# Where two expert biases are added, who adds a tile's first weighted row, and when half a block's stores start

## The reference

```python
combine, dispatch = top2_dispatch(z_g, Wg, C)        # 24 experts, 4 groups of 256 tokens, C = 22
disp = einsum('sec,sd->ecd', dispatch, x)
h    = einsum('ecd,edf->ecf', disp, W1) + b1[:, None, :]     # 128 -> 512
hid  = relu(layer_norm(einsum('sec,ecf->sf', combine, h)))   # back to tokens, normalised
y    = einsum('ecf,efd->ecd', einsum('sec,sf->ecf', dispatch, hid), W2) + b2[:, None, :]
out  = layer_norm(z + einsum('sec,ecd->sd', combine, y))
```

## Time and profile before

| | us |
|---|---|
| three runs | 425.24, 430.27, 430.97 (median 430.27) |
| profiled execution | 429.6 |
| its span on the core | 427.9 |
| granted TensorE clock, mean | 0.941 |
| busy in the span: PE, DVE, ACT, POOL | 381.2, 263.7, 192.8, 117.2 |

### The profile page before, as it was taken

How to read it: one execution, slowest core, us unless ns; L and a number is a source line. 1 busy time by engine, 2 the same in 40 slices (tenths; PEclk the granted TensorE clock), 3 DMA queues, 4 the chain that set the end, 5 groups by cost and what they waited for, 6 DMA issues and landing times.

```text
span 427.9 us, 7077 instructions
## 1 busy us (share of the span) xinstructions
PE 381.2 (89%) x2675; PEld 216.7 (51%) x2675; DVE 263.7 (62%) x682; ACT 192.8 (45%) x303; POOL 117.2 (27%) x160
## 2 busy tenths in 40 slices
PE   8998968999897999999998899987997897999961
PEld 3675447874343232333332585644575332788951
DVE  4777703325788789889823886626168637893435
ACT  5323102310506567776787596655625541533200
POOL 4013785460507146100110000110000055744042
PEclk9995997999999799999999999996899998999976
DMA  4499514014167444000000000005999487322132
GB/s 116 134 141 330 210 44 115 30 44 113 37 185 191 106 121 103 3 1 3 2 3 0 2 1 2 0 0 204 389 294 290 159 264 227 121 79 63 41 81 55
DMA packets 35877, 46.03 MB, mean 108 GB/s; under 512 B 4778, under 2 KB 21682, under 8 KB 35844
## 3 DMA queue, kind: packets, MB, share of 16 engines
q1 hardware_dynamic: 33156, 38.57, 32.0%
q0 software_dynamic: 2688, 7.02, 5.9%
HBM read 31.67 MB, written 13.78 MB: 106 GB/s over the span
## 4 chain that ended last, share of the span: by engine, by line
PE 58%; DVE 12%; issue 8%; DMA 6%; ACT 6%; POOL 4%; another core or an unknown queue 4%; POOLq 0%; SPq 0%; DVEq 0%; ACTq 0%
PE ps L1438 7%; PE ps L1694 7%; PE ps L1680 7%; PE ps L1655 6%; PE ps L1990 4%; PE ps L1663 3%; PE ps L2015 2%; PE ps L1943 2%; PE ps L1852 2%; PE ps L1799 2%; POOL y_d L593 2%; PE ps L1442 2%; PE ps L1808 2%; PE ps L1599 2%
## 5 line engine op out<-in xcount | busy, mean ns | idle before, releaser
L1255 DVE TENSOR_REDUCE early<-ps 128x1 f32<-128x512 f32 x128 | 81.6, 685 | 13.2 <-PE ps L1655 9.8
L812 ACT ACTIVATE R<-ps 128x1024 f32<-128x1024 f32 x64 | 62.6, 1019 | 23.9 <-PE ps L1680 23.0
L1680 PE MATMUL ps<-R 75*128 75x512 bf16 x128 | 38.8, 391 | 2.2 <-DMA R<-R 2.1
L1655 PE MATMUL ps<-R 72*128 72x512 bf16 x112 | 39.2, 392 | 0.8 <-DVE early L1255 0.8
L1438 PEld LDWEIGHTS ps<-ident,R 128*77 128x77 f32 (+1 forms) x216 | 24.2, 145 | 23.1 <-issue 9.9
L663 POOL DMA_INDIRECT R<-h_d,srow x16 | 15.4, 963 | 73.8 <-DMA h_d<-ff 67.6
L1438 PE MATMUL ps<-ident,R 128*77 128x128 f32 (+1 forms) x216 | 31.7, 280 | 4.2 <-ACT R L804 1.8
L1694 PE MATMUL ps<-R,vaug 128*9 128x512 f32 x256 | 34.3, 609 | 0.6 <-ACT R L812 0.6
L1442 PE MATMUL ps<-early,ones_b 128*128 128x512 bf16 (+1 forms) x119 | 30.6, 403 | 1.6 <-POOL ident L532 1.6
L1655 PEld LDWEIGHTS ps<-R 72*128 72x128 bf16 x112 | 11.0, 98 | 32.5 <-DVE early L1255 19.6
L1221 DVE TENSOR_SCALAR R<-ps,vcol 128x256 f32<-128x256 f32 x16 | 7.0, 479 | 25.2 <-remote 13.4
(11 more groups left out here) (340 smaller groups left out, 717.6 us busy)
## 6 DMA issues: line engine op xcount, KB each, us to landing
R<-in_L_ffn_W_dram SPq DMA_DIRECT2D x1, 6144.0 KB, 19.7
h_d<-R SPq DMA_DIRECT2D x12, 256.0 KB, 4.7
q_d<-R SPq DMA_DIRECT2D x24, 96.0 KB, 1.9
R<-k_d SPq DMA_DIRECT2D x24, 96.0 KB
R<-q_d SPq DMA_DIRECT2D x8, 288.0 KB
R<-in_L_ffn_w_dram SPq DMA_DIRECT2D x1, 2048.0 KB
h_d<-ff SPq DMA_DIRECT2D x6, 256.0 KB, 4.6
disp_d<-R SPq DMA_DIRECT2D x1, 1032.0 KB, 13.0
```

What stands on the lines that cost most here:

```text
L812: s.activation(probs[idx % 4], ps[:, 2 * (idx % 2):2 * (idx % 2) + 2, :].rearrange("p b t -> p (b t)"), ACT.Exp, scale=QK_SCALE).then_inc( ...
L1255: v.tensor_reduce(mcol[:, u, col:col + 1], bank(ring_bank("row", n)), AX.X, ALU.max).then_inc(s1_max, 1)
L1655: m.matmul(bank(ring_bank("row", n)), Q9[0:KQ, b, h, t * P:(t + 1) * P], K9[0:KQ, b, h, :], start=True, stop=True).then_inc(s1_mm, 1)
L1680: ins = m.matmul(bank(2 * (idx % 2) + j), K9[0:KM, b, h, kt * P:(kt + 1) * P], Q9[0:KM, b, h, :], start=True, stop=True)
```

## The change

- b1 is added to quads 0 to 11 by DVE as it copies them, from `b1rep`, each expert's row repeated over its 32 slots' partitions (six loads of 256 KB). `DVE_QUADS` is now 0 to 11; the copies stand inside the routing: block 0's after the one-hots, block 1's after the row indices for the gathers. In quads 12 to 17, which ACT copies, PE adds b1 by one bf16 matmul per quad (`quad_bias`: three parts of b1 times `of_slot`, which ACT builds; POOL splits b1 in parts during the attention). `hidden_bias`, the transposes of combine and ACT's copies of them are gone.
- b2 is added by DVE in the copies of output blocks, from `b2rep` (six loads of 64 KB). ACT copies no blocks; `output_bias` and DVE's additions of it are gone.
- SP issues the twelve loads between W1 and W2, after the last projection.
- ACT makes the first weighted row of tiles 1 to 7 in PSUM (`inner_part`); DVE does it for tile 0. The root takes epsilon as its bias, and L1394 is gone.
- SP waits before the store of quad 9 (second half of block 1) until tiles 0 and 1 are gathered.
- POOL splits tile 0 right after the gathers of tile 2, DVE splits tile 1 itself.
- The transposes of the last group's weights stand ahead of the hidden groups. ACT's evacuations and roots are interleaved anew.
- The output groups are finished in the order 0, 3, 1, 2; blocks 1 and 2 are copied by DVE after group 0.

```diff
-DVE_QUADS = (6, 8)
+DVE_QUADS = tuple(range(12))
...
-BIAS_BANK = (5, 4) * 4
-LAST_BANK = (6, 7, 1)
+PART_BANK = (4, 5)
+LAST_BANK = (0, 6, 7)
+KB = 96
...
+        b1rep = [v[:, F1 * i:F1 * (i + 1)] for v in (
+            flat(attn), wx[:, :, :].rearrange("p w d -> p (w d)"), vaug[:, :, :, :].rearrange("p t h d -> p (t h d)")) for i in range(2)]
+        b1_parts = wx_qk[0:KB, :, :].rearrange("p w d -> p (w d)").bitcast(BF16)
+        of_slot = bias[0:KB, R_QV:R_SO + 1, :].rearrange("p r d -> p (r d)").bitcast(BF16)
...
-        out_order = (0, 1, 3, 2)
+        out_order = (0, 3, 1, 2)
...
+            sp.wait_ge(proj_mm, 2 * B)
+            for quad in range(QUADS):
+                sp.dma_start(b1rep[quad], a["L1_ffn_b1"][4 * quad:4 * quad + 4, :].unsqueeze(1).to_broadcast([4, 32, F1])).then_inc(ld_rep, 16)
+            for quad in range(QUADS):
+                sp.dma_start(b2rep[:, D * quad:D * (quad + 1)],
+                             a["L1_ffn_b2"][4 * quad:4 * quad + 4, :].unsqueeze(1).to_broadcast([4, 32, D])).then_inc(ld_rep, 16)
...
+                if blk == 1 and s == 3:
+                    for q in (0, 1):
+                        sp.wait_ge(gathered[paired[q]], 32)
...
-                if q == 3:
+                if q == 2:
                     last_rest(0)
-                    last_rest(1)
...
-                s.activation(tmp8[:, q:q + 1], tmp8b[:, q:q + 1], ACT.Sqrt).then_inc(hstd, 1)
+                s.activation(tmp8[:, q:q + 1], mv[:, q, 1:2], ACT.Sqrt, bias=eps6[:, :]).then_inc(hstd, 1)
+            def inner_part(q):
+                t = paired[q]
+                act.wait_ge(gathered[t], 32)
+                if q == 1:
+                    act.wait_ge(gates_ready, 1)
+                if q >= 2:
+                    act.wait_ge(hvar, q - 1)
+                s.activation(bank(PART_BANK[q % 2]), got1[q % 4][:, 0, :], ACT.Copy, scale=gate[1][:, 0, t:t + 1]).then_inc(hpart, 1)
...
-            for i in range(QUADS):
-                copy_quad(i)
+            act.wait_ge(proj_mm, 2 * B)
+            for part in range(3):
+                rows = slice(32 * part, 32 * part + 32)
+                ins = s.copy(of_slot[rows, :].rearrange("p (e c) -> p e c", c=32),
+                             ident[rows, 32 * part:32 * part + E1].unsqueeze(2).to_broadcast([32, E1, 32]))
+            ins.then_inc(of_slot_ready, 1)
             evac_slots1(2)
-            for b in range(B):
-                act.wait_ge(comb_tp, b + 1)
-                s.copy(combT[:, b * SEQ:(b + 1) * SEQ], ps[0:E1, 4 + b, :]).then_inc(combT_ready, 1)
+            evac_slots1(3)
...
-            def copy_block(blk, part):
-                act.wait_ge(y1_mm, 2 * blk + part + 1 + (B if blk else 0))
-                for half in range(2):
-                    wait_half_stored(act, BLOCKS - 1, half)
-                s.copy(yblock[blk][part], ps[:, BLOCK_BANK[blk] + part, 0:(4, 2)[part] * D]).then_inc(y1_act, 1)
-            def copy_quads(first, last):
-                for i in range(first, last + 1):
-                    copy_quad(i)
-            copy_quad(7)
-            copy_quads(9, 11)
-            evac_slots1(3)
-            copy_quads(12, 13)
+            copy_quad(12)
+            copy_quad(13)
+            inner_part(1)
             hid_std(0)
-            copy_quads(14, 16)
+            copy_quad(14)
+            copy_quad(15)
+            copy_quad(16)
             hid_std(1)
             copy_quad(17)
+            copy_last(0)
+            inner_part(2)
+            evac_hidden(0)
             hid_std(2)
-            for c in range(4):
-                evac_hidden(c)
+            inner_part(3)
+            evac_hidden(1)
+            evac_hidden(2)
             hid_std(3)
-            for i in range(3):
-                copy_last(i)
+            evac_hidden(3)
+            copy_last(1)
+            copy_last(2)
+            inner_part(4)
+            evac_hidden(4)
             hid_std(4)
-            for c in range(4, 7):
-                evac_hidden(c)
+            inner_part(5)
+            evac_hidden(5)
+            evac_hidden(6)
             hid_std(5)
             evac_hidden(7)
+            inner_part(6)
             hid_std(6)
-            copy_block(0, 0)
-            copy_block(0, 1)
+            inner_part(7)
             hid_std(7)
             for c in range(8, 15):
                 evac_hidden(c)
-            copy_block(1, 0)
-            copy_block(1, 1)
             for i, gr in enumerate(out_order):
-                if i == 1:
-                    copy_block(2, 0)
-                    copy_block(2, 1)
...
+            def copy_quads(first, last):
+                dve.wait_ge(ld_rep, 16 * 2 * QUADS)
+                for i in range(first, last):
+                    blk, slot = i // QUADS, i % QUADS
+                    dve.wait_ge(h1_mm, i + 1)
+                    if blk >= 1:
+                        wait_half_stored(dve, blk - 1, slot // 3)
+                    v.tensor_tensor(ring[slot], bank(W1_BANKS[i % 3]), b1rep[slot], ALU.add).then_inc(h1_dve, 1)
...
                     one_hot_slots()
+                    copy_quads(0, QUADS)
...
                     v.tensor_tensor(growh[:, :, :], to_slot, col1, ALU.add).then_inc(grow_ready, 1)
+                    copy_quads(QUADS, 2 * QUADS)
...
+            for q in range(T):
+                t = paired[q]
+                inner, rest = hsum[q % 6], hrest[q % 6]
+                partial = bank(PART_BANK[q % 2])
+                if q == 0:
+                    dve.wait_ge(gathered[t], 32)
+                    me.link(v.tensor_scalar(partial, got1[0][:, 0, :], g1[:, 0, t:t + 1], None, ALU.mult))
+                else:
+                    dve.wait_ge(hpart, q)
+                if q >= 6:
+                    dve.wait_ge(hdisp_mm, 4 * ((q - 6) // 2 + 1))
+                me.link(v.scalar_tensor_tensor(out=inner, in0=got1[q % 4][:, 1, :], scalar=g1[:, 1, t:t + 1],
+                                               in1=partial, op0=ALU.mult, op1=ALU.add))
+                me.link(v.bn_stats(st6[:, q, :], inner))
+                v.bn_aggr(mv[:, q, :], st6[:, q, :]).then_inc(hvar, 1)
+                dve.wait_ge(hstd, q + 1)
+                me.link(v.reciprocal(rstd[:, q:q + 1], tmp8[:, q:q + 1]))
+                me.link(v.tensor_scalar(inner, inner, mv[:, q, 0:1], rstd[:, q:q + 1], ALU.subtract, ALU.mult))
+                v.tensor_tensor(rest, inner, top(inner), ALU.subtract).then_inc(hid_r1, 1)
+                if q == 1:
+                    dve.wait_ge(hid_r1, 2)
+                    v.tensor_tensor(hlast[1], rest, top(rest), ALU.subtract).then_inc(hid_p3, 1)
...
-            for i in DVE_QUADS:
...
-                v.tensor_copy(ring[slot], bank(W1_BANKS[i % 3])).then_inc(h1_dve, 1)
-            for q in range(T):
...
-                dve.wait_ge(hb_mm, q + 1)
...
-                me.link(v.scalar_tensor_tensor(out=partial, in0=got1[q % 4][:, 0, :], scalar=g1[:, 0, t:t + 1],
-                                               in1=partial, op0=ALU.mult, op1=ALU.add))
...
-                v.tensor_scalar(tmp8b[:, q:q + 1], mv[:, q, 1:2], MOE_EPS, None, ALU.add).then_inc(hvar, 1)
...
-            add_bias_rows()
+            def copy_block(blk):
+                for part in range(2):
+                    dve.wait_ge(y1_mm, 2 * blk + part + 1)
+                    for half in range(2):
+                        wait_half_stored(dve, BLOCKS - 1, half)
+                    columns = (4, 2)[part] * D
+                    v.tensor_tensor(yblock[blk][part], ps[:, BLOCK_BANK[blk] + part, 0:columns],
+                                    b2rep[:, 4 * D * part:4 * D * part + columns], ALU.add).then_inc(y1_dve, 1)
+            copy_block(0)
...
+                if i == 1:
+                    ins.then_inc(gates_ready, 1)
+                    dve.wait_ge(gates_ready, 1)
+                else:
+                    me.link(ins)
             for b in range(B):
...
+            def quad_bias(i):
+                wait_quad_copied(pe, i - 3)
+                m.matmul(bank(W1_BANKS[i % 3]), of_slot[:, P * (i % QUADS):P * (i % QUADS + 1)], b1_parts, start=True, stop=False)
...
-            pe.wait_ge(comb_ready, 1)
-            for t in range(T):
-                ins = tp(ps[0:E1, 4 + t // TB, (t % TB) * P:(t % TB + 1) * P], comb[:, t, :], P)
-                if t % TB == TB - 1:
-                    ins.then_inc(comb_tp, 1)
             first_product(1, 0)
             first_product(1, 1)
             dispatch(3)
-            pe.wait_ge(ld_hid, 32)
-            hidden_bias(0)
-            first_product(2, 0)
-            hidden_bias(1)
-            first_product(2, 1)
-            hidden_bias(2)
-            hidden_bias(3)
-            for i in range(BLOCKS * QUADS - 3, BLOCKS * QUADS):
+            pe.wait_ge(bias_parts, 1)
+            pe.wait_ge(of_slot_ready, 1)
+            last = BLOCKS * QUADS
+            for i in range(last - QUADS, last - QUADS + 3):
+                quad_bias(i)
```

(79 more changed lines are left out.)

44 lines of the change are left out of this document (10 added, 34 removed).

## The result

The changed kernel takes 444.22 us (median of four runs, 442.97 to 448.24), the kernel before, run beside it, 430.62 us (median of four). The ratio is 1.037, 95% interval 1.027 to 1.048: slower, where 426.0 us was forecast with a range up to 433.0. The profiled execution took 448.24 us, 3.5 us above the next slowest run.

A forecast was written before the change was run, and what follows sets the result against it. Bound by TensorE, almost without holes from 371.52 us, behind a DMA relay: -3.9 (biases) +0.7 (second group) = -3.2 mid-kernel, -5.1 at the end; 429.6 - 5.1 + 0.7 (median) + 0.8 (waits) = 426.0 us, range 420.5 to 433.0.

The forecast's parts named there:

- The loads of repeated rows: SP's queue between the two weights: twelve loads take 4.1 + 1.3 us, second weights land at 339.1 instead of 333.7.
- The queue: SP's queue: first stores wait behind the second weights, first gather at 344.5 instead of 343.00, +1.5 us.
- Held stores: SP before quad 9: block 1's stores land +4.3 us later, shrunk to +0.7 at the first hidden group.
- rival that the hold becomes the limit: SP before quad 9: second hidden group at 375.5 uses up the 3.9 us gained; 434.4 us, chance 0.10.
- Second group: Second hidden group on TensorE: starts at 372.2 against 371.52, +0.7 us, with VectorE at 3.4 us per tile.
- Middle sum: TensorE from second hidden group to block 1's products: these start at 393.0 against 396.16, -3.2 us.
- The tail: Block 2's products to the end: thin stretch gone, last gathers in time, VectorE ends at 420.6 against 425.67, -5.1 us.
- bursts: Last 18 matmuls of block 2, issued unevenly before the change; forecast to vanish as TensorE ends before the gathers.
- the 4 us: Block 2's products: time lost before the change against 28 ns per matmul, forecast to be won back.
- the thin stretch: TensorE's slow last products of block 2, forecast gone; the rival that it stays gave 431.1 us, chance 0.28.
- the 2.7 of the sum: The 24 sum products at the end: 2.7 us at 2.4 GHz instead of 5.39 at half clock.
- The slower case: Rival with SP's hold before quad 9 as limit and the thin stretch kept: 434.4 us, chance 0.10.

The follow-up runs named there:

- e1: Changed kernel with the same repeated bias rows in 16 loads of slowest dimension 32 instead of 12 of slowest dimension 4: 1.015 of before.
- e2: Changed kernel without SP's wait ahead of quad 9's store: 1.032 of before.
- e3: e1 without SP's wait ahead of quad 9's store: 1.012 of before.
- e12: e9 without SP's wait ahead of quad 9's store: 1.006 of before.
- e8: Kernel before plus only the six b1 loads (slowest dimension 4, data unused) between first and second weights: 1.035 of before.
- e11: Kernel before plus only the b1 rows, unused, in twelve loads of slowest dimension 32 ahead of the second weights: 1.010 of before.
- e5: e1 with VectorE's copies of block 1 ahead of output group 0 instead of behind it: 1.007 of before.
- e9: e5 with the b2 rows loaded behind the stores of block 1 instead of ahead of the second weights: 1.003 of before.

## Why the prediction was wrong

The step that failed is the price of "The loads of repeated rows". It took 1.57 MB at 387 GB/s and 0.39 MB at 295 GB/s, 5.4 us, as if any DMA filled all engines. From the first weights' issue to the second weights' landing the changed kernel took 19.6 us more than before (61.8 against 42.2). The upper bound for the first gather, +5.4, rested on that rate (the lower one, 0, on stores that pass), so the range held no case near the truth. e1 puts 10.2 us of the 19.6 on the form and leaves the rest to the bytes: 1.97 MB, every copy of a row counted (the profile lists 256 KB for a load of four rows of 2 KB), at the 239 GB/s of e1 are 8.2 us. Why these rows of 2 KB go at 239 GB/s and those of the first weights at 387 no run shows. The Trainium skill (DMA: Bandwidth & Descriptors, Why a DMA increments its semaphore by 16 and not by 1, How many engines) says that the slowest dimension of each side that isn't 1 is looked at and the largest number up to 16 that divides both is taken: 4 for `[4, 32, 512]`, 16 for `[32, 2, 512]`. The trace agrees (a share of 0.27 against 1.05 to 1.10). By that rule, as an estimate, the twelve loads come to 4 times the 5.4 us, 21.6, close to the 19.6 measured. It stood in the page I cited for another rule, and the shape stood in the diff.

The other steps, by their own numbers:

- **The queue.** Right: stores wait behind the second weights. With the loads at their true price it passed 14.9 of the 19.6 us on to the first gather, where +1.5 was forecast, and the end came 16.5 us later (table).
- **Held stores.** Right in size: first hidden group 17.4 us after the first gather, 17.3 forecast. The rival that the hold becomes the limit fell (e2, e3, e12).
- **Second group.** 28.7 us after the first gather, 27.7 forecast. VectorE needs 3.4 to 3.6 us per tile, as said. Its wait of 3.37 us for tile 2's weighted row is the gather's: ScalarE had itself waited 4.95 us for the rows, which landed 5.20 us after the second gather's issue, where the prediction took 3.6 to 4.2. The wait of 2.62 us for tile 4's root is ScalarE's order: the root stands behind an evacuation that waits for TensorE. POOL, ACT and DVE in the changed kernel:

```profile
373.35 0.99 POOL L682 DMA_INDIRECT R<-h_d,srow  x1 [5.42 <-DMA h_d<-ff]
...
379.87 0.69 ACT L937 ACTIVATE ps<-R,gate 128x512 f32<-128x512 f32 x1 [4.95 <-DMA R<-h_d,srow]
...
380.59 0.75 DVE L1417 SCALAR_TENSOR_TENSOR attn<-R,gate,ps 128x512 f32<-128x512 f32 x1 [3.37 <-ACT ps L937]
...
392.64 0.16 DVE L1422 RECIPROCAL rstds<-tmp 128x1 f32<-128x1 f32 x1 [2.62 <-ACT tmp L928]
```

- **Middle sum.** From the second group to block 1's products 24.2 us (388.77 to 412.94), 20.8 forecast. The 3.9 us of bias matmuls are gone, but a hidden group at half clock, an evacuation and longer products took back 3.4. TensorE had waited ahead of that group, so the wait was paid twice, once as time and once as clock.
- **The tail.** Right: no bursts, sums in 2.94 us. Wrong: that this belongs to the change. e8 and e11, the old program but for loads, have 336 products in 9.38 us and the sums in 2.95 and 2.94, too. So the 4 us go without the change, and crediting them to it was the second mistake. They were also overrated: from the second group to the end the profile of before has 56.3 us and that of e11, without the thin stretch, 54.5, that is 1.8 less and not the 4 and the 2.7 of the sum. (By the prediction's own terms TensorE would end at 408.5 - 3.2 = 405.3, not 405.6; it changes nothing.) Wrong also: that the last gathers come in time with the block copies behind group 0. These copies start the eight gathers late, 1.25 us each on POOL, which then set the end (e5 against e1 3.8 us, against e3 4.1).
- **Rivals.** The slower case ended at 434.4 us and named the hold. None priced a DMA by its shape.

With the loads of e11 costing 1.0% and e9, which has the same loads ahead of its stores, at 1.003, the rest of the change is worth about 0.7% once its tail is mended. The uncertainty of that difference is 1.0%, so whether the forecast gain of 4.3 us (1.0%) was in the change can't be told.

It stays open why VectorE took up the sums 2.8 us late in the changed kernel's profile (in e1, after 0.05 us), and what the hold is worth.
